# Attention by pairs of heads: unsplit fp32 weights times values in column halves, scores in row halves, denominators from added blocks

## What is computed

```python
def taylor_exp(x):
    x2 = (x[..., :, None] * x[..., None, :]).reshape(*x.shape[:-1], FD * FD) / R2
    return jnp.concatenate([jnp.ones_like(x[..., :1]), x / RRD, x2 / RD], axis=-1)
...
A_qk = jnp.tril(jnp.einsum('bhnd,bhmd->bhnm', q_f, k_f))
y1 = jnp.einsum('bhnm,bhme->bhne', A_qk, v)
A_qk2 = jnp.einsum('bhnd,bhmd->bhnm', q_f, k_enc_f)
y2 = jnp.einsum('bhnm,bhme->bhne', A_qk2, v_enc)
k_state = k_enc_f.sum(axis=2, keepdims=True) + jnp.cumsum(k_f, axis=2)
z = 1.0 / ((q_f * k_state).sum(axis=-1) + EPS)
out = (y1 + y2) * z[..., None]
...
x = _layernorm(x + attention(x)); x = _layernorm(x + experts(x))
```

## Time and profile before

| | us |
|---|---|
| median of 3 runs | 1237.49 |
| lowest and highest | 1235.59, 1238.7 |
| span of the profiled execution | 1235.0 |
| busy: PE | 1111.0 |
| busy: DVE | 755.0 |
| busy: ACT | 734.6 |
| busy: POOL | 586.8 |

### The profile page before, as it was taken

One profiled execution on the slowest core, in us unless ns is written; L12 is line 12 of the kernel. 1 busy time (PEld: TensorE's weight loads), 2 busy tenths in 40 slices (PEclk: granted clock), 3 DMA queues, 4 the chain that ended last, 5 costly groups with the idle time before them and its releaser, 6 DMA issues. The chain is left out here.

```text
span 1235.0 us, 20482 instructions
## 1 busy us (share of the span) xinstructions
PE 1111.0 (90%) x5392; PEld 842.0 (68%) x5393; DVE 755.0 (61%) x1010; ACT 734.6 (59%) x1220; POOL 586.8 (48%) x871
## 2 busy tenths in 40 slices
PE   5999999999999999999999999994279999999994
PEld 4677767877776776786777677673246667776663
DVE  5586678578578667857857866784514334333442
ACT  1697599489669759948966975991023333233331
POOL 2375367158347536715834753551114444444442
PEclk8999999999999989999999999996589999999998
DMA  5230231131133024013113202312570011100010
GB/s 165 75 77 18 63 104 25 53 104 45 43 87 74 18 59 107 22 53 104 45 43 88 73 18 71 82 35 81 229 313 27 29 34 33 34 31 30 26 33 2
DMA packets 43014, 81.93 MB, mean 66 GB/s; under 512 B 14974, under 2 KB 19072, under 8 KB 40674
## 3 DMA queue, kind: packets, MB, share of 16 engines
q1 hardware_dynamic: 39234, 72.19, 20.2%
q0 software_dynamic: 3744, 9.31, 2.5%
HBM read 35.30 MB, written 9.31 MB: 36 GB/s over the span
## 5 line engine op out<-in xcount | busy, mean ns | idle before, releaser
L303 POOL TENSOR_SCALAR_AFFINE_SELECT raw<-raw 128x128 f32<-128x128 f32 (+1 forms) x384 | 260.6, 695 | 214.7 <-ACT raw L352 212.4
L490 DVE SCALAR_TENSOR_TENSOR weights_l<-raw,weights_h 128x1024 fp32r<-128x1024 f32 (+1 forms) x256 | 293.0, 1147 | 96.6 <-ACT weights_h L361 92.2
L352 ACT ACTIVATE raw<-slot 128x1024 f32<-128x1024 f32 (+1 forms) x256 | 231.5, 910 | 12.3 <-PE slot L662 9.6
L676 PE MATMUL osum<-weights_h,values_h 128*96 128x512 f32 (+3 forms) x640 | 217.5, 343 | 11.5 <-DVE weights_l L490 10.3
L677 PE MATMUL osum<-weights_h,values_l 128*64 128x512 f32 (+3 forms) x640 | 210.9, 330 | 0.0
L678 PE MATMUL osum<-weights_l,values_h 128*96 128x512 f32 (+3 forms) x640 | 208.6, 334 | 0.0
L662 PE MATMUL slot<-qop,kop 128*128 128x512 f32 (+3 forms) x640 | 167.9, 365 | 32.4 <-ACT raw L352 25.8
L1085 ACT ACTIVATE active<-upT,b 128x128 f32<-128x128 f32 x312 | 84.7, 382 | 158.1 <-PE upT L1163 158.1
L662 PEld LDWEIGHTS slot<-qop,kop 128*128 128x128 f32 x640 | 109.3, 193 | 70.6 <-ACT raw L352 42.4
L1139 PE MATMUL down<-w,active 128*128 x624 | 143.8, 384 | 2.5 <-ACT active L1085 2.4
L1151 PE MATMUL up<-w,rowsT 128*128 x312 | 142.5, 600 | 0.7 <-ACT rowsT L1074 0.7
(11 more groups left out here) (139 smaller groups left out, 1494.5 us busy)
## 6 DMA issues: line engine op xcount, KB each, us to landing
w<-in_w SPq DMA_DIRECT2D x16, 1024.0 KB, 9.4
kop<-kh SPq DMA_DIRECT2D x128, 80.0 KB, 2.0
kop<-kl SPq DMA_DIRECT2D x128, 80.0 KB, 2.1
qop<-qh SPq DMA_DIRECT2D x256, 32.0 KB, 1.9
qop<-ql SPq DMA_DIRECT2D x256, 32.0 KB, 2.0
y<-in_xT SPq DMA_DIRECT2D x8, 512.0 KB, 3.6
raw<-in_x SPq DMA_DIRECT2D x8, 512.0 KB, 3.3
attention_rows<-y SPq DMA_DIRECT2D x8, 512.0 KB, 2.9
```

The lines of the kernel that those rows point to most:

```text
L303: pool.affine_select(out=w, in_=w, compare_op=ALU.is_ge, fill=-0.5, base=0, pattern=[[0, blocks], [1, P]], channel_multiplier=-1).then_inc ...
L352: act.activation(raw[:, h % 2, a:b], slot[half][:, 0:b - a], ACT.Square, bias=HALF_ROOT).then_inc(squared, 1)
L490: dve.scalar_tensor_tensor(weights_l[:, h % 2, a:b], src, 0.5, weights_h[:, h % 2, a:b].bitcast(F32), ALU.add, ALU.subtract).then_inc(part ...
L676: pe.matmul(dst[:, q0:N], vh, wh, start=(half == 0 and n == 0), stop=False)
```

## The change

The attention is rewritten; the experts are not touched. What it does:

- The unit is a pair of heads n. Its two heads stand in the two halves of the partitions of `kop` and `qop` (64 rows each). SP fills them with 16 DMAs of 16 partitions (8 for `kop`, 8 for `qop`); four pairs fit (`RING` = 4). The two heads' scores are matmuls of 64 rows, one in the upper and one in the lower half of the array's rows, into two banks of PSUM.
- The 1792 columns are four units u of 512, 512, 512 (128 + 384) and 256 columns for both heads. A gap g is a quarter of a pair; a batch has 32. ACT squares a unit of both heads at once, DVE adds the half, on the cut columns together with a mask (`scalar_tensor_tensor`), and weights and values are plain fp32, one matmul a block, 64 columns, the two heads in the two column halves of the array.
- POOL adds the blocks of weights of a pair into `wsum` (four additions), and PE multiplies them by a column of ones that stands at the pair's row (`onehot`); all denominators of a batch gather in one bank `den`.
- The denominators of a batch leave by DRAM: copied, stored, loaded as 128 x 64, inverted, stored, and loaded back as rows over 64 partitions for each head, two pairs of buffers (`INV` = 2). DVE multiplies, a batch later. All these DMAs are on SP.
- Projections, output, turning and router are pieces that share one bank `piece`, each piece waiting for the one before to be read (`PIECE_NO`), at the gaps of the tables below. x is split by DVE, not POOL, and has a tile of its own.
- The loop over the batches is unrolled.

```diff
+UNITS, GAPS, WIDTH = 4, 32, 1792
+UNIT_BLOCKS = [[(NT, 0, 0)], [(0, 0, 0)], [(3, 384, 0), (1, 128, 128)], [(2, 256, 0)]]
+RING, ATT, INV = 4, 12, 2
+V_LATE_AT = {0: 0, 2: 1, 4: 2, 6: 3, 8: 4}
+QK_AT = {13: 0, 15: 1, 17: 2, 19: 3, 21: 4}
+OUT_AT = {14: 0, 16: 1, 18: 2, 20: 3}
+V_EARLY_AT = {22: 0, 23: 1, 24: 2, 25: 3, 26: 4}
+TURN_AT, ROUTER_AT = {28: 0, 29: 1}, 30
+XH_GAP, XL_GAP = 9, 11
+INVERT_GAP, NORM_GAP, MOMENTS_GAP, CENTRE_GAP, RSTD_GAP = 3, 6, 22, 25, 23
...
         @block.sync
...
+            def gather(b, p):
+                m, r = p // 4, 32 * (p % 4)
+                n = b * PAIRS + p
+                if p % 4 == 0:
+                    sp.wait_ge(piece_read, nth(b, "qk", 2 if m == 0 else 4) + 1)
+                if n >= RING:
+                    sp.wait_ge(scored, UNITS * (n - RING) + UNITS)
+                for s in range(2):
+                    for c in range(4):
+                        i, f = HD * s + FD * c, r + FD * s
+                        sp.dma_start(kop[i:i + FD, n % RING, :].bitcast(F32),
+                                     (kh, kl, kh, kl)[c][f:f + FD, m, :].bitcast(F32)).then_inc(op_ready[n % RING], 16)
+                        sp.dma_start(qop[i:i + FD, n % RING, :].bitcast(F32),
+                                     (qh, ql, ql, qh)[c][f:f + FD, m, :].bitcast(F32)).then_inc(op_ready[n % RING], 16)
+            def spread_den(b):
+                sp.wait_ge(den_copied, b + 1)
+                sp.dma_start(den_rows[0:PAIRS, :], den_sb[0:PAIRS, :]).then_inc(den_out, 16)
+                sp.dma_start(den_rows[PAIRS:H, :], den_sb[HD:HD + PAIRS, :]).then_inc(den_out, 16)
+                sp.wait_ge(den_out, 32 * (b + 1))
...
+                sp.dma_start(den2[:, :], den_rows.rearrange("h (c n) -> (h c) n", n=H * N // P)).then_inc(den_in, 16)
+            def store_inverse(b):
+                sp.wait_ge(inverted, b + 1)
...
+                sp.dma_start(inv_rows.rearrange("h (c n) -> (h c) n", n=H * N // P), den2[:, :]).then_inc(inv_out, 16)
+                sp.wait_ge(inv_out, 16 * (b + 1))
+            def load_inverse(b, p):
+                n = b * PAIRS + p
+                if n >= INV:
+                    sp.wait_ge(normalised, n - INV + 1)
+                for s in range(2):
+                    sp.dma_start(inv[HD * s:HD * s + HD, n % INV, :],
+                                 inv_rows[PAIRS * s + p, :].partition_broadcast(HD)).then_inc(inv_loaded[n % INV], 16)
...
+            for p in range(RING):
+                gather(0, p)
             sp.dma_start(wo[:, :, :], wo_in).then_inc(small_loaded, 16)
...
+            for b in range(B):
+                if b + 1 < B:
+                    load_x(b + 1)
+                gather(b, 4)
+                if b > 0:
+                    spread_den(b - 1)
+                gather(b, 5)
+                if b > 0:
+                    store_inverse(b - 1)
+                    for p in range(4):
+                        load_inverse(b - 1, p)
+                gather(b, 6)
+                if b > 0:
+                    for p in range(4, PAIRS):
+                        load_inverse(b - 1, p)
+                gather(b, 7)
+                if b + 1 < B:
+                    for p in range(3):
+                        gather(b + 1, p)
+                if b > 0:
+                    store_rows(b - 1)
+                if b + 1 < B:
+                    gather(b + 1, 3)
+                if b > 0:
+                    load_rows(b)
...
         @block.scalar
...
+            def high_qk(b, i):
+                act.wait_ge(piece_full, nth(b, "qk", i) + 1)
+                if i == 0 and b > 0:
+                    for r in range(RING):
+                        act.wait_ge(op_ready[r], 256 * b * PAIRS // RING)
...
         @block.vector
...
+            def finish_weights(n, u):
+                src = w[:, n % 2, :, UNIT_AT[u]:UNIT_AT[u] + UNIT_COLS[u]]
+                cut = (0, P, 2 * P, P)[u]
+                dve.wait_ge(squared, UNITS * n + u + 1)
+                if cut:
+                    dve.scalar_tensor_tensor(src[:, :, 0:cut], src[:, :, 0:cut], 0.5,
+                                             mask[:, 0:cut].unsqueeze(1).to_broadcast([P, 2, cut]), ALU.add,
+                                             ALU.mult).then_inc(w_ready, 1)
+                dve.tensor_scalar(src[:, :, cut:], src[:, :, cut:], 0.5, None, ALU.add).then_inc(w_ready, 1)
+            def normalise(n):
+                dve.wait_ge(inv_loaded[n % INV], 32 * (n // INV + 1))
+                dve.wait_ge(att_copied, n + 1)
...
         @block.tensor
...
+            def output(b, t):
+                take_piece(b, "out", t)
+                if t == 0:
+                    pe.wait_ge(normalised, PAIRS * (b + 1))
...
+            def scores(n, u):
+                if u == 0:
+                    pe.wait_ge(op_ready[n % RING], 256 * (n // RING + 1))
+                if UNITS * n + u >= 2:
+                    pe.wait_ge(squared, UNITS * n + u - 1)
+                for j, q0, col in UNIT_BLOCKS[u]:
+                    for s in range(2):
+                        last = pe.matmul(slot[u % 2][:, s, col:col + N - q0],
+                                         kop[HD * s:HD * s + HD, n % RING, j * P:j * P + P],
+                                         qop[HD * s:HD * s + HD, n % RING, q0:N], start=True, stop=True,
+                                         skip_group_check=True)
+                last.then_inc(scored, 1)
+            def weigh(n, u):
...
+                for j, q0, col in UNIT_BLOCKS[u]:
+                    for s in range(2):
+                        h, at = 2 * p + s, UNIT_AT[u] + col
+                        last = pe.matmul(osum[n % 2][HD * s:HD * s + HD, q0:N], values[:, j, h * HD:h * HD + HD],
+                                         w[:, n % 2, s, at:at + N - q0], start=(u == 0), stop=(u == UNITS - 1),
+                                         skip_group_check=True)
...
+            for b in range(B):
+                for g in range(GAPS):
+                    n, u = b * PAIRS + g // UNITS, g % UNITS
+                    if n + 1 < B * PAIRS:
+                        scores(n + 1, u)
+                    weigh(n, u)
+                    if u == DEN_UNIT:
+                        denominators(n)
+                    if g in V_LATE_AT:
+                        project_values(b, 1, V_LATE_AT[g])
+                    if b + 1 < B and g in QK_AT:
+                        project_qk(b + 1, QK_AT[g])
+                    if b > 0 and g in OUT_AT:
+                        output(b - 1, OUT_AT[g])
```

More of the change, by code:

```diff
@@ L444, in _ @@
+            copy_att(B * PAIRS - 1)
         @block.vector
@@ L577, in _ @@
+            invert(B - 1)
+            for p in range(PAIRS):
+                normalise((B - 1) * PAIRS + p)
+            for t in range(NT):
+                residual(B - 1, t)
             moments(B - 1)
-            normalise(B - 1)
-            turned_rows(B - 1)
+            centre(B - 1)
+            copy_turned(B - 1, 0)
+            copy_turned(B - 1, 1)
             logits_of(B - 1)
@@ L586, in three @@
                 parts = [(wh, vh), (wh, vl), (wl, vh)]
-                for n, (a, b) in enumerate((a, b) for a in range(3) for b in range(KD)):
-                    last = pe.matmul(dst, parts[a][0](b), parts[a][1](b), start=(n == 0), stop=(n == 3 * KD - 1))
-                return last
-            def take(it, u):
-                if u >= 2:
-                    pe.wait_ge(slot_free[u % 2], it * FREED + u // 2)
-                elif not (isinstance(it, int) and it == 0):
-                    pe.wait_ge(squared, it * (2 * H))
@@ L598, in turn_rows, with take_piece @@
-            def turn_rows(b):
-                pe.wait_ge(y_ready, b * NT + NT)
-                pe.wait_ge(copied, b * (2 * H) + 2 * H)
+                for n, (a, k) in enumerate((a, k) for a in range(3) for k in range(KD)):
+                    last = pe.matmul(dst, parts[a][0](k), parts[a][1](k), start=(n == 0), stop=(n == 3 * KD - 1),
+                                     skip_group_check=True)
+                return last
+            def take_piece(b, kind, i):
+                if nth(b, kind, i) > 0:
+                    pe.wait_ge(piece_read, nth(b, kind, i))
@@ new lines, in output, with turn_rows @@
+            def output(b, t):
+                take_piece(b, "out", t)
+                if t == 0:
+                    pe.wait_ge(normalised, PAIRS * (b + 1))
+                for p in range(PAIRS):
+                    last = pe.matmul(piece[:, 0:D], att[:, (b * PAIRS + p) % ATT, t * P:t * P + P], wo[:, p, :],
+                                     start=(p == 0), stop=(p == PAIRS - 1))
+                last.then_inc(piece_full, 1)
+            def turn_rows(b, k):
+                take_piece(b, "turn", k)
+                if k == 0:
+                    pe.wait_ge(y_ready, NT * (b + 1))
+                for n in range(4):
+                    t, c = 2 * k + n // KD, n % KD
```

(38 more changed lines are left out.)

711 lines of the change are left out of this document (283 added, 428 removed).

## The result

The changed kernel takes 1465.4 us (median of 4 runs, 1462.9 to 1467.6), the one before 1237.5 beside it: ratio 1.184, 95% interval 1.181 to 1.186. Forecast were 1414 us in a range of 1355 to 1480: the sign and the mechanism hold, the size is 51 us short, and about 42 of these lie in the six full batches, each of which is some 7 us longer than forecast.

The account below looks back on a forecast made before the run. PE's own stream bounds the kernel before; SP's queue would bound the changed one. Start 77.7, batch 0 84, 7 extra, six batches of 119, last 101, end 48: attention 1034 with rounding, plus 377.0 and 2.5: 1414 us, range 1355 to 1480.

Parts of the forecast that it names:

- SP's queue sets the batch: Attention batches: SP's ordered issues, ACT's wait for the last gather and PE's work behind it close a cycle; batch 119 us.
- Gathers at 0.633: SP's q and k copies issue 0.633 us apart whatever their partitions; 16 a pair take 10.13 us, 81 a batch.
- SP's part, 68.6 to the last issue and 2.0 of landing: SP in each batch: five gathers, denominators' and inverses' trips and inverse loads sum to 68.6 us; the last gather lands 2.0 later.
- The bound that the text names for an issue of 0.63: SP's loads of inverses: issuing at 0.63 us instead of the assumed 0.47 would add 8 us.
- PE from the first output to gap 27, 44.9 and 2.0 for the clock: PE behind the wait: outputs 13.8, q/k 5.5, values 7.0, pair work 18.6, sum 44.9 us; 2.0 more for a lower clock.
- Overlap with in-order starts: PE's fp32 weights-times-values: second head's first record runs beside the first head's second; a lone unit lasts three records, 1.29 us.
- No drain at a switch: PE: changing between whole array, row halves and column halves costs nothing, since starts stay 0.23 us apart across 64-column matmuls.
- rival 2: PE: each form switch exposes a 0.17 us tail; 36 switches add 6 us a batch, +45, 1460 us; chance 0.07.
- Start 77.7, batch 0 84, first full batch 7 longer, last 101, end 48: Attention's edges in us: time to first weigh with clock, first batch, late SP entry, batch 7, closing steps after it.
- PE 87 us a batch, DVE and POOL 88 by excluding each other: Busy time per batch: PE's own stream 87 us; DVE's excluding part 38 plus POOL's 50 together 88, not longer than PE.
- Rival 3: SP's 16-partition copies issue at 0.37 us like full ones; DVE and POOL hold batches at about 104, 1285 us; chance 0.05.
- Rival 4: SP keeps ahead and PE stays the bound: 87 us a batch, attention 797, total 1177 us; chance 0.04.

Follow-up runs that it names:

- 8 copies: Changed kernel with each gather as 8 copies of 32 partitions instead of 16 of 16, same bytes, wrong rows: 1300.3 us.
- four buffers: Changed kernel with four buffers for the inverses instead of two: 1421.0 us.
- merged loads: Changed kernel with everything that relieves SP together, and one broadcast load of a pair's inverses instead of two: 1443.3 us.
- the series: Changed kernel with extra 12-round sequences of matmuls in different array forms ahead of batch 0; round distances were read, for example 0.858 us for column halves.
- the run with 4 copies: Changed kernel with each gather as 4 copies of 64 partitions instead of 16 of 16, same bytes, wrong rows: 1279.8 us.
- kernel with 8 copies and the right rows: Changed kernel with operand rows reordered so one copy of 32 partitions with a step of 4 serves both heads, results right: 1302.3 us.
- finer wait: Changed kernel where ACT's first q copy waits only for pairs 0 to 3 and the third piece for the rest: 1394.2 us.
- small loads first: Changed kernel with the loads of wo, wr, br and zero rows ahead of the first gathers on SP: 1461.6 us.

## Why the prediction was right, step by step

- **SP's queue sets the batch**: right, and shown from both sides. Taking its issues away (8 copies), its stops (four buffers) or the wait on it (two lines) each shortens the batch; an earlier start of PE is mostly lost again, and 21.8 us more of PE's work a batch lengthen it by 9.8 only. POOL's sums were taken away only where the merged loads held the batch, which says nothing of after.
- **Gathers at 0.633**: right, 10.1 us a pair. **SP's part, 68.6 to the last issue and 2.0 of landing**: measured 74.0, 3.4 more. Mis-sized were the inverses: I took 0.47 a load, by a row between two kinds, and it is 0.64, with a landing of 2.9 instead of 2.0. The blocks took 6.6 and 8.9 for 5.5 and 6.0, 4.0 more; the gathers 1.3 more in all; the two trips were 0.9 and 0.8 shorter. The bound that the text names for an issue of 0.63 is +8 in total, which was far too low: 4.0 us a batch are 24 over the six full batches. A part of it is the landing, for which the text had a bound of its own (3 us, +35).
- **PE from the first output to gap 27, 44.9 and 2.0 for the clock**: measured 50.2 (618.1 to 668.3), 3.3 more. Two terms were wrong and nearly cancelled. *Overlap with in-order starts* fell: the halves overlap fully, 1.5 us a pair or 4.4 in this stretch less. *No drain at a switch* (rival 2 at 0.07) fell too: 36 switches at 0.17 to 0.2 are 6 to 7 more. So what rival 2 says of PE was true, at its own price of 0.17 and against its chance of 0.07. That its 1460 us lie nearer to the 1465 than the forecast is luck in part: the overlap took 4.4 a batch off, and the loads of the inverses put 4.0 on. The bound "full overlap 8 less" doesn't follow from the forecast's own prices either, by which it is 4.4 a batch, some 26 in six. The clock cost 2.8 on the first output (6.51 where undisturbed ones take 3.72), not 2.0. The step that failed is the reading of L677 between L676 and L678: those are fp32r matmuls of 64 columns, and the series show that such a one costs no switch (0.469 a round), while an fp32 one of 64 columns does. The row was right and bore on another case. The Trainium skill's rule of the drain (TensorEngine Tiling (Array Packing), Key Properties) agrees with the series, and gives no figure; I had given it too little.
- **Start 77.7, batch 0 84, first full batch 7 longer, last 101, end 48**: measured 79.7, 86.9, 8.6 longer, 102.4, 52.2. The end is 4 off: inverses at 0.64 again (the four rounds took 15 us, 12.5 forecast) and a first output at the lower clock (5.23 against 3.72).
- **PE 87 us a batch, DVE and POOL 88 by excluding each other**: PE is busy for 93.1 in the run with 4 copies. By the prices of the series a pair is 0.82 + 3.5 x 0.86 + 0.86 + 8 x 0.17 = 6.1, the 6.2 of the forecast by other terms; missing were the switches around the 22 whole-array pieces, 22 x 0.2 = 4.4 a batch: 8 x 6.1 + 37.4 + 4.4 = 91. POOL's 6.2 a pair is 6.45 at the rate it was read from, and measured are 6.5. In after it was not DVE and POOL that set the batch; a product stretched beside POOL (1.76 us at 601.7 us for 0.69) is a part of SP's second block. In the run with 4 copies a part of it does: the wait of 4.2 us for the low part of x.
- **Rival 3** (1285 with the copies cheap): the run with 4 copies, whose gathers cost even less, gave 1280, and 102 a batch for its 104. What holds that batch is in part what the rival names, DVE beside POOL and the inverses.
- **Rival 4** (faster if SP keeps ahead): its 1177 us are refuted by the same run, for PE alone is busy for 93 us a batch and not 87. That the kernel would stay above 1237 isn't shown: in that run, 3.4% above before, PE's waits for the low parts of q (behind SP) and of x (DVE beside POOL) are 17.9 and 26.8 us in all, together as much as the 42 that it lacks, and the rival's own sum with 93 us a batch would give some 1225. The kernel with 8 copies and the right rows shows, in its profiled execution of 1306.5 us, where the time goes against the kernel before: start +17, batch 0 -23, six batches +25 (106.6 to 107.6 each), last batch +24, end +26 (52.1 for 25.6), together 70 in the attention. A middle batch has 93 to 94 us of PE's work for 97 and is no shorter, and both ends are longer; at the last one nothing is left to hide the trip of the inverses through DRAM.

No version that was run is faster than the kernel before; the fastest that computes the right numbers takes 1302 us. Whether the relief without the merged load (finer wait, four buffers, small loads first, 8 copies) would come near 1237 was not run. The end alone takes 26 us more than before.

## What to carry to other kernels

Count the issues on a queue before the bytes: a copy costs its 0.6 us whether it moves 32 or 160 KB, so look for a layout in which one copy with a step over partitions does the work of two. Follow the queue in its written order, through the waits, and close the cycle; then engines that are busy for three quarters no longer mislead. Look for a second branch that ends just before the first, for it caps what a change on the first can give. Where a wait asks for all of something, see which part it needs: here it was half, and two lines gave back 71 us.

## What the runs showed of the hardware

- A switch between whole array, row halves and column halves costs 0.17 to 0.20 us of TensorE each (512 columns, granted clock 1.00). fp32 next to fp32r in the same form costs nothing. A 64-column fp32r matmul between whole-array ones is no switch (0.469 us for the two), where a 64-column fp32 one is (1.433).
- Two fp32 matmuls in the two column halves, and two fp32r ones in the row halves, start within 0.01 us and overlap fully: 0.858 and 0.234 a pair of 512 columns.
- A copy within SBUF issues in 0.59 (0.63 from start to start) with 16, 32 or 64 partitions; the median landing grows from 2.0 us at 32 or 40 KB to 2.4 to 2.6 at 128 or 160 KB.
- A broadcast load written with an outer dimension of 2 released its readers 5.1 us apart and stopped the issuing queue for up to 8.3 us a load; two of the 16 DMA engines were busy meanwhile (share 0.13). Two loads of half the partitions each issue in 0.6.
